# Order of routing, last attention steps and tile tables between the batch stage and the expert stage of a decoder layer

## The reference

```
x = layernorm(x + linear_attention(x))          # softmax over q's features and k's tokens, 16 heads
x = layernorm(x + cross_attention(x, ctx))      # 16 heads of 16
g = gelu(x @ wg1 + bg1);  probs = softmax(g @ wg2)          # 64 hidden, 8 experts
top_vals, top_idx = top_k(probs, 2);  gates = those two probabilities, 0 elsewhere
h = gelu(einsum('nd,edh->enh', x, w_in));  o = einsum('enh,ehd->end', h, w_out)
x = layernorm(x + einsum('ne,end->nd', gates, o))           # 256 -> 512 -> 256 in each expert
```

## Time and profile before

| what | us |
|---|---|
| device time, median of 3 runs | 425.37 |
| lowest and highest of the 3 | 425.27, 427.67 |
| span of the profiled execution, first to last instruction | 412.1 |
| PE busy in the span | 339.6 |
| DVE, ACT, POOL busy | 308.5, 221.7, 218.5 |

### The profile page before, as it was taken

One profiled execution on the slowest core, in us unless ns is written; L12 is line 12 of the kernel. 1 busy time (PEld: TensorE's weight loads), 2 busy tenths in 40 slices (PEclk: granted clock), 3 DMA queues, 4 the chain that ended last, 5 costly groups with the idle time before them and its releaser, 6 DMA issues. The chain is left out here.

```text
span 412.1 us, 12355 instructions
## 1 busy us (share of the span) xinstructions
PE 339.6 (82%) x4025; PEld 275.9 (67%) x4025; DVE 308.5 (75%) x913; ACT 221.7 (54%) x518; POOL 218.5 (53%) x287
## 2 busy tenths in 40 slices
PE   1977999999999999999988763798999999999100
PEld 0656777777777878777767542577889999887000
DVE  2866988888888988888878876687888665655193
ACT  3425676666667666667666654452554454443043
POOL 8335446766676666757535885745133323422183
PEclk9998999999999999999989995699999999999855
DMA  7710222202220122202102222427353222311493
GB/s 225 225 45 1 79 80 79 77 2 79 80 78 13 69 78 80 69 12 79 52 2 68 94 93 70 168 74 255 107 133 87 85 79 80 100 51 36 164 357 127
DMA packets 21387, 38.43 MB, mean 93 GB/s; under 512 B 3696, under 2 KB 11120, under 8 KB 21328
## 3 DMA queue, kind: packets, MB, share of 16 engines
q1 hardware_dynamic: 16768, 26.11, 20.6%
q0 software_dynamic: 3408, 9.44, 6.3%
q10 hardware_dynamic: 1152, 2.10, 1.4%
HBM read 24.75 MB, written 12.89 MB: 91 GB/s over the span
## 5 line engine op out<-in xcount | busy, mean ns | idle before, releaser
L586 POOL DMA_INDIRECT parts<-QKT,rows_all x39 | 37.7, 967 | 74.9 <-DVE QKT L1221 69.4
L328 PE MATMUL bank<-QS,EW 128*128 128x256 f16 (+1 forms) x384 | 59.6, 257 | 1.5 <-DVE XB L1034 1.5
L492 POOL TENSOR_TENSOR rstd<-veps,neghalf 128x1 f32<-128x1 f32 x48 | 38.1, 794 | 36.0 <-DVE veps L857 35.5
L1397 PE MATMUL bank<-EW,QV 128*128 x312 | 48.7, 273 | 2.3 <-DVE R L1213 1.1
L1213 DVE TENSOR_TENSOR R<-scratch,QV 128x512 f16<-128x512 f32 x39 | 26.7, 691 | 30.3 <-ACT scratch L776 18.2
L328 PE MATMUL bank<-XB,EW 128*128 128x256 f16 (+1 forms) x192 | 47.4, 256 | 0.0
L776 ACT ACTIVATE scratch<-bank 128x512 f32<-128x512 f32 x39 | 23.4, 601 | 39.8 <-PE bank L328 39.8
L328 PEld LDWEIGHTS bank<-QS,EW 128*128 x384 | 36.6, 98 | 6.6 <-issue 2.1
L1139 DVE TENSOR_REDUCE NM<-bank 128x4 bf16<-128x512 f32 x64 | 39.5, 678 | 1.3 <-PE bank L1552 1.2
L507 POOL DMA_INDIRECT bkt<-REC,dest x32 | 32.5, 1017 | 12.8 <-issue 8.4
L710 ACT ACTIVATE rows_all<-bank 128x512 f32<-128x512 f32 x64 | 33.2, 604 | 8.0 <-PE bank L1586 8.0
(11 more groups left out here) (240 smaller groups left out, 933.9 us busy)
## 6 DMA issues: line engine op xcount, KB each, us to landing
scratch<-w_in SPq DMA_DIRECT2D x8, 512.0 KB, 3.7
scratch<-w_out SPq DMA_DIRECT2D x8, 512.0 KB, 3.4
rows_all<-bkt SPq DMA_DIRECT2D x15, 264.0 KB, 3.3
XC<-x SPq DMA_DIRECT2D x16, 128.0 KB, 3.5
XC<-ctx SPq DMA_DIRECT2D x16, 128.0 KB, 3.4
EW<-parts SPq DMA_DIRECT2D x8, 256.0 KB, 6.6
EW<-parts ACTq DMA_DIRECT2D x8, 256.0 KB, 7.4
out<-rows_all SPq DMA_DIRECT2D x8, 256.0 KB, 2.1
```

Source lines behind the costliest of these rows:

```text
L328: last = pe.matmul(dst, a(c), b(c), start=(c == 0 and i == 0), stop=(c == n - 1 and i == 2))
L492: pool.tensor_tensor(rstd[n][p][:], veps[n][p][:], neghalf[:, 0:1], ALU.pow).then_inc(s_rs[n], 1)
L586: pool.indirect_dma_start(parts, bass.IndirectOffsetOnAxis(ap=home[:, t, f:f + 1], axis=0), Y[t % 2][:, f, :], None).then_inc(s_put[t % 2] ...
L1397: last = pe.matmul(bank[4 + t % 2][:, f * D:(f + 1) * D], a[t % 2][:, h, f * P:(f + 1) * P], b[:, h, :], start=(h == 0 and i == 0 and f == 0),
```

## The change

It changes orders only; no instruction is added or taken away.

- SP: the row numbers of tiles 0 to 2 are read into registers ahead of the wait for group 0's scatters, those of tiles 3 to 6 ahead of the wait for the other groups' scatters. The wait on s_pv asks for batch 14 instead of 15.
- POOL: `pw2:14` goes from behind `sc:15` to behind `sc:11`, `pw2:15` from behind `sc:18` to behind `sc:16`.
- ACT: `X2T:14` goes ahead of `gelu:1`, `X2T:15` behind `second:1` (it was ahead of it).
- DVE: `n2:14` goes ahead of `O2T:15`, `choice1:1` and `choice2:1` ahead of `n2:15`, `choice2:2` ahead of `low:0`. whole_tiles(0) and (1) go into the tail, before and after `low:1`, whole_tiles(2) to where whole_tiles(0) was; `whose:0` and `whose:1` go from the tail into round 0. The table work of round 1 goes to round 2, ahead of whose(3).
- PE: `x2T:14` goes ahead of `ao2:15`, `cnt:1` ahead of `x2T:15`, `cnt:2` ahead of `upa:0`.

```diff
@@ sync
-            def tile_load(t):
+            def first_of(t):
+                return sp.value_load(base[0:1, t:t + 1], min_val=0, max_val=NE * CAP)
+
+            def tile_load(t, first=None):
...
-                first = sp.value_load(base[0:1, t:t + 1], min_val=0, max_val=NE * CAP)
+                first = first_of(t) if first is None else first
...
-            sp.wait_ge(s_pv, 4 * NB)
+            sp.wait_ge(s_pv, 4 * (NB - 1))
             sp.wait_ge(s_tables, 1)
+            firsts = [first_of(t) for t in range(FULL)]
             sp.wait_ge(s_scat[0], 16 * 2 * EARLY)
             for t in range(FULL):
-                tile_load(t)
+                tile_load(t, firsts[t])
             sp.wait_ge(s_tables, 2)
+            firsts = [first_of(t) for t in range(FULL, NX)]
             for g in range(1, NG):
                 sp.wait_ge(s_scat[g], 16 * 2 * (EDGE[g + 1] - EDGE[g]))
             for t in range(FULL, NX):
-                tile_load(t)
+                tile_load(t, firsts[t - FULL])
@@ gpsimd
-"sc:11 past_mT:15 sc:12 sc:13 past_sc:15 sc:14 sc:15 pw2:14 sc:16 sc:17 past_pv:15 sc:18 pw2:15 sc:19 "
+"sc:11 pw2:14 past_mT:15 sc:12 sc:13 past_sc:15 sc:14 sc:15 sc:16 past_pv:15 pw2:15 sc:17 sc:18 sc:19 "
@@ scalar
-"X2T:13 lns:15 rec:15 gcp:13 gelu:1 X2T:14 exps:1 X2T:15 second:1 gcp:15 gelu:2 high:0 "
+"X2T:13 lns:15 rec:15 gcp:13 X2T:14 gelu:1 exps:1 second:1 X2T:15 gcp:15 gelu:2 high:0 "
@@ vector
-"... R2:14 s2:14 O2T:15 nr:15 full:1 R2:15 s2:15 n2:14 "
-"choice1:1 n2:15 choice2:1 full:2 gate1:1 dest:1 gate2:1 full:3 "
-"choice1:2 low:0 choice2:2 whose:0 gate1:2 dest:2 gate2:2 low:1 whose:1")
+"... R2:14 s2:14 n2:14 O2T:15 nr:15 full:1 R2:15 s2:15 choice1:1 choice2:1 "
+"n2:15 full:2 gate1:1 dest:1 gate2:1 full:3 "
+"choice1:2 choice2:2 low:0 gate1:2 dest:2 gate2:2 whole:0 low:1 whole:1")
...
             hidden_low(0)
-            whole_tiles(0)
+            whole_tiles(2)
             for t in range(MAXT):
                 if t == FULL - 1:
                     tile_low(FULL)
+                    tables_of_round(t - 1)
                     whose(FULL)
...
                 if t == 0:
-                    whole_tiles(1)
+                    whose(0)
                 if t + 1 < MAXT:
                     hidden_low(t + 1)
                 if t == 0:
-                    whole_tiles(2)
+                    whose(1)
...
-                tables_of_round(t)
+                if t != FULL - 2:
+                    tables_of_round(t)
@@ tensor
-"cntpre:1 gh:13 ao2:15 lg:1 x2T:14 x2T:15 gh:15 cnt:1 cntpre:2 lg:2 turn:0 upa:0 cnt:2 turn:1 upb:0")
+"cntpre:1 gh:13 x2T:14 ao2:15 lg:1 cnt:1 x2T:15 gh:15 cntpre:2 lg:2 turn:0 cnt:2 upa:0 turn:1 upb:0")
```

More of the change, by code:

```diff
@@ L1187, in emit @@
                     full_tiles(b)
+                if step == "whole":
+                    whole_tiles(b)
                 if step == "low":
@@ L1199, in _ @@
                      "mx0:14 n1:15 mx1:14 mx2:14 mx3:14 R2:12 s2:12 O2T:13 nr:13 QM1:15 full:0 n2:12 mx0:15 mx1:15 mx2:15 "
[3 rows of a table removed]
+                     "mx3:15 R2:13 s2:13 ewl:15 O2T:14 nr:14 n2:13 ewl:16 R2:14 s2:14 n2:14 O2T:15 nr:15 full:1 R2:15 s2:15 choice1:1 choice2:1 "
+                     "n2:15 full:2 gate1:1 dest:1 gate2:1 full:3 "
+                     "choice1:2 choice2:2 low:0 gate1:2 dest:2 gate2:2 whole:0 low:1 whole:1")
             def hidden_low(t):
```

## The result

The changed kernel took 431.46 us in the median of four runs, against 426.22 for the kernel before beside it (425.27 to 427.67). One of the four took 1919 us, which no later comparison repeated; without it the three lie between 429.35 and 431.94, median 430.97. The ratio, which leaves that run out, is 1.0107, 95% interval 1.006 to 1.0153: slower by 4.6 us, where 1.8 us faster was forecast. The profiled execution's span is 427.6 us.

What follows compares the result with a forecast made beforehand. PE was taken as the bound, full from 284 to 380 us, so entering that stretch earlier counts whole. Gains 1.0 + 0.1 + 0.65 = 1.8 us off the median 425.37 gave 423.6 us, range 422.1 to 425.2.

Steps and rivals of the forecast that it cites:

- row numbers ready: End of the table work on DVE for tile 0's load: at 252.2, 2.9 us earlier than before.
- SP's first load: Issue of tile 0's load on SP: at 255.0 (bounds 255.0 and 255.7), against 256.31 before.
- the next two loads apart: Sign on SP: the two loads after tile 0's come 0.4 us apart instead of 1.1.
- `sc:19`'s landing: Group 0's last scatter, landing at 254.9, replaces the table as the last thing tile 0's load waits for.
- Three reads in a row: SP's row-number reads for tiles 0 to 2: taken as 2.6 us, bounds 1.1 and 3.4.
- tile 3's wait: PE's wait for the DMA loading tile 3 goes: 0.65 us gained, bounds 0 and 0.65.
- A: Rival: `sc:19` or tile 0 lands late, gain smaller, 424.6 us; chance 0.18.
- B: Rival: PE's clock comes back later after `upa:0`, slower, 426.1 us with 5 us more low clock; chance 0.09.
- C: Rival: PE's clock comes back earlier, up products at full clock, 1.2 us more gained, 422.4 us; chance 0.14.
- these 13.3: Base: median 425.37 lies 13.3 us above the profiled span of 412.1; taken as fixed, gains subtracted from the median.
- `cnt:2`, three matmuls ... moves into PE's wait: 0.1 us gained: On PE, group 2's counts move from between upa and `turn:1` into the wait before `upa:0`: 0.1 us gained.
- 1.0 us: Tile 0's load lands earlier, `turn:0` begins at 258.0 instead of 259.02; bounds a loss of 0.3, a gain of 1.3.

Runs made afterwards that it cites:

- e2: The changed kernel again, in a session where the kernel before takes 414 us: 411.32 us, ratio 0.9944.
- e1: The kernel before again, nothing changed, in a session where it takes 414 us: 413.88 us, ratio 0.9999.
- e3: The kernel before with only SP's row numbers read ahead of the waits, in a session where before takes 414 us: 417.95 us, ratio 1.0103.
- k4: The kernel before with only `cnt:2` ahead of `upa:0` on PE and `choice2:2` ahead of `low:0` on DVE: 431.01 us, ratio 1.0108.
- k1: The changed kernel with `cnt:2` behind `upa:0` on PE again and whole:0 behind `low:1` on DVE: 424.54 us, ratio 0.9956.
- k2: The changed kernel with one more wait on POOL, `sc:28` waiting for ACT's `high:1`: 424.06 us, ratio 0.9958.
- g1: The kernel before, unchanged, profiled in a session where it takes 425 us: 425.59 us, ratio 1.0011.
- g4: The changed kernel again, in a session where the kernel before takes 425 us: 428.51 us, ratio 1.0074.
- k3: The changed kernel with one more wait on POOL, `sc:26` waiting for `turn:1`'s signal: 425.12 us, ratio 0.9963.
- e6: The changed kernel with whole_tiles, whose and tables_of_round where the kernel before had them: 432.4 us, ratio 1.0162.
- l1: The changed kernel with PE, ACT and DVE in the order of before; POOL's powers, tables and reads stay early: 423.75 us, ratio 0.9935.

## Why the prediction was wrong, and where it was right

**The mechanism that it priced is there.** In the 414 session e2's batch stage ran 1.30 us ahead of e1's (X1T at 227.01 and 228.31); with that added back:

| step | forecast | e2 + 1.30 |
|---|---|---|
| row numbers ready | 252.2 | 252.0 |
| SP's first load | 255.0 | 255.0 |
| the next two loads apart | 0.4 | 0.52 (three in 1.38) |
| `turn:0` | 258.0 | 258.1 |
| first up product | 260.6 | 260.7 |
| wait for tile 3's DMA | none | none |

The table came 3.0 us earlier than in e1 (forecast 2.9) and was no longer last; `sc:19`'s landing was, as forecast. Three reads in a row took 2.2 us (e3: 254.51 to 256.69), four took 2.4 to 2.5, where 2.6 and 3.0 were put in. The page "DMA: Bandwidth & Descriptors" of the Trainium skill gives a floor of some 600 ns for a tensor_load (section Latency and other measured facts). If that is the price of a read like these, which the page doesn't say, the trace agrees: 2.43 / 4 = 0.61. From the first up product on, the forecast had 0.65 for tile 3's wait. e1 has 0.60 us for tile 3's DMA there and 0.48 for DVE's QKT right behind it, and e2 neither. The second wait isn't in the forecast; that it followed from the first is likely and not shown. Forecast 1.8, measured 2.7 (0.9944, interval 0.9924 to 0.9964).

**Rivals A, B and C.** `sc:19` and tile 0 landed as priced (tile 0 in 3.1 us). After PE had begun the up products at low clock, they ran at 0.11 us each again by 265.0 in e1 and by 262.5 in e2, 3.3 and 3.1 us later, so neither B nor C happened there. In the first comparison the 8 us without work and the low clock are effects of the held signal: PE is at 0.50 in tile 0's products as before, is at 0.50 again behind the wait (282.8 to 286.0), and runs at 1.00 from 298 on.

**What failed, first: the base.** "I take these 13.3 as fixed" was wrong. Only 1.8 us lie outside the span. The remaining 11.5 us were a sign that the profiled execution and the timed ones were not doing the same, and they lay in the very stretch that the change reorders. A gap between span and median that no launch cost explains should have been a rival of its own.

**Second: the step "`cnt:2`, three matmuls ... moves into PE's wait: 0.1 us gained".** That is all that it was priced at, on PE. In a 425 session this step costs what k4 shows, 4.6 us (1.0108 x 426 - 426); taken out of the change (k1) or covered by a pause (k2) it turns 1.0074 into 0.9956 and 0.9958. What it releases is gates and destinations of group 2, and through them POOL's `sc:28` to `sc:31`, which close the pause in the row of scatters that 425 sessions have. The forecast did reckon that scatters come earlier, but only as transfers beside tile 0's load and as the landing that tile 3's load waits for. It could not have read this price off its rows: they are of a 414 us execution, in which the row has no pause to close (257.49 to 271.41 in steps of 1.27) and nothing is held. So the base is the root of the miss, and this step is where it cost.

**Third: "1.0 us" at tile 0** is not to be seen in the first comparison. There the table was ready at 261.96 against 262.81 in g1, only 0.85 earlier; the three reads then take 2.17 us instead of the 1.16 to g1's load at 263.97, and `turn:0` starts at 267.04 against 266.72. The batch stage ahead is held too (ACT's waits for "remote" of 2.2, 2.9 and 2.8 us at 234, 244 and 254), as it is in g1. But these executions weren't level before (X1T at 229.25 against 228.44); counted from there `turn:0` is 0.5 us earlier, in g4 0.8, and in k1 and k3, whose orders are the same up to `turn:0`, 1.9 and 2.0 later. Whether the 1.0 us comes in a 425 session stays open.

The accounts close to within the scatter of single profiles. In both kinds of session the span is `high:1` plus 145.1 to 148.9 us in 18 of the 20 profiles (146.8 for e1, 146.9 for g1, 146.3 for g4, 146.4 for k2); the other two are e3 and e6, with their 2.65 us of waiting for tile 3 (150.0 and 150.2). g4 against g1: `high:1` 4.2 us later, the rest 0.6 shorter (g1 waits 0.6 us for tile 3's DMA, g4 not at all), together 3.6 in the spans and 2.9 in the medians.

**Still open.** Why sessions differ, and what in the chip holds the signal. In a 425 session the trace also keeps fewer landings (the scatters' row of the DMA view has a median time in e1 and none in g1), so whatever delays the signals may also be what thins the records. Whether a device that isn't profiled shows the hold wasn't tried. Nor is it known what starts it: in the first changed run the row of scatters begins at 264.28, the results of `turn:0` (267.04) and `cnt:2` (268.60) came through, and that of `turn:1` (272.20) did not. Nor is it known what ends the shorter holds of the batch stage, which end within a row. That the place of the pause decides when `high:1` runs is shown by k1, k2 and k4; that the hold comes from the scatters' traffic, rather than from POOL's work of issuing them, is not.

## What to carry to other kernels

Before working out a difference of a per cent, compare the profiled span with the timed median: the 13 us between them, of which only 1.8 lie outside the span, meant here that two regimes were mixed, and the stretch where they part is where the reordering cost. When a step is moved forward, follow what it releases on every queue to the end, above all on POOL, and on a profile of the kind that is timed: work that fills a pause there can be dearer than the pause. Reading row numbers ahead of waits pays only when the table they come from is early; alone it cost 4 us.

## What the runs showed of the hardware that was not expected

In the 425 sessions ACT's use of `turn:1`'s result waited until POOL's unbroken row of indirect DMAs was through. Over all 15 runs of that kind `high:1` started 0.8 to 2.2 us after the row's last instruction ended, while those ends ranged from 272.3 to 281.5 us. In 14 of them it came 3.0 (l1) to 9.2 us (the first changed run) behind the start of `turn:1`; in the fifteenth, k3, `turn:1` began after the row's end and `high:1` followed in 0.8 us. In the 414 session, with the same unbroken row in e2, it came 0.75 us behind it. What is held is PE's outgoing signals, to ACT and DVE alike (k1: both go on at 277.30), while DVE's signal to PE took 0.05 us in such a stretch. It isn't a matter of the row alone: the results of `turn:0` pass early in the row, and holds of 2 to 3 us in the batch stage end within one. The hold at `high:1` can outlast everything that PE has left to do, and then the clock is low as well when the work resumes (granted clock 0.50 from 282.8 to 286.0 in the first changed run).
